# Eighty sampling steps in one pipeline, an expert network in tiles of chosen rows, one attention pipeline for all batches

## The reference

```python
x = x + deformable_attention(ctx, layernorm(x))   # 16 heads of 8, 5 points per head
x = x + moe0(layernorm(x))        # 32 experts of width 96, top 4 by sigmoid score + bias
x = x + attention1(layernorm(x), ctx)             # softmax over 154 tokens, then a norm
x = x + moe1(layernorm(x))        # 8 experts of width 512, top 2 by 20 Sinkhorn iterations

def moe0(x):                                       # all 2048 tokens
    scores = sigmoid(x @ gate_w.T)
    ids = top_k(scores + e_bias, 4)
    w = scores[ids] / sum(scores[ids])
    return sum over e: (silu(x @ w1[e]) * (x @ w3[e]) * combine[:, e]) @ w2[e]
```

## Time and profile before

| what | us |
|---|---|
| median of 3 runs | 1264.88 (1264.18 to 1271.11) |
| the profiled execution's own time | 1261.6 |
| its span, first to last instruction | 1259.7 |
| PE busy | 868.3 (69%) |
| DVE busy | 784.9 (62%) |
| ACT busy | 414.7 (33%) |
| POOL busy | 307.0 (24%) |
| mean granted TensorE clock | 0.843 of full |

### The profile page before, as it was taken

How to read it: one execution, slowest core, us unless ns; L and a number is a source line. 1 busy time by engine, 2 the same in 40 slices (tenths; PEclk the granted TensorE clock), 3 DMA queues, 4 the chain that set the end, 5 groups by cost and what they waited for, 6 DMA issues and landing times.

```text
span 1259.7 us, 13989 instructions
## 1 busy us (share of the span) xinstructions
PE 868.3 (69%) x4534; PEld 493.6 (39%) x4534; DVE 784.9 (62%) x1888; ACT 414.7 (33%) x731; POOL 307.0 (24%) x287
## 2 busy tenths in 40 slices
PE   4276589775689977667998667699684233269993
PEld 2022345322355432235554223454342122158883
DVE  2767655787776467777647686764583766744434
ACT  1122212133424633342463334336442111124441
POOL 2822100332600033250003134200100900036662
PEclk9988689988779997887999788699978555579997
DMA  6254000164000016500000750000050000001114
GB/s 218 86 187 148 16 0 1 55 214 161 13 3 1 1 37 218 176 1 16 1 1 21 233 174 3 4 1 1 26 183 9 1 0 1 0 23 41 43 43 117
DMA packets 45893, 77.94 MB, mean 62 GB/s; under 512 B 6599, under 2 KB 30413, under 8 KB 45438
## 3 DMA queue, kind: packets, MB, share of 16 engines
q1 hardware_dynamic: 43326, 71.91, 17.2%
q0 software_dynamic: 2496, 5.12, 1.5%
HBM read 71.76 MB, written 5.24 MB: 61 GB/s over the span
## 4 chain that ended last, share of the span: by engine, by line
PE 52%; DVE 30%; ACT 8%; issue 4%; DMA 3%; POOL 1%; SPq 1%; another core or an unknown queue 0%; DVEq 0%; POOLq 0%; PEldq 0%; ACTq 0%
PE PS L1280 6%; PE PS L1289 5%; PE PS L1402 5%; PE PS L1294 4%; DVE oh L954 4%; PE PS L1397 3%; PE PS L1661 3%; PE PS L1411 3%; PE PS L1639 2%; DVE oh L955 2%; PE PS L1302 2%; DMA oh<-index 2%; PE PS L1644 2%; DVE pkr L914 2%; PE PS L1516 1%
## 5 line engine op out<-in xcount | busy, mean ns | idle before, releaser
L1397 PE MATMUL PS<-oh,T 128*128 128x512 bf16 x240 | 80.5, 453 | 121.8 <-DVE oh L954 121.7
L794 DVE TENSOR_TENSOR sg<-sg,PS 128x512 f32<-128x512 f32 x96 | 66.0, 687 | 135.3 <-ACT sg L592 76.4
L617 ACT COPY gs<-PS 128x512 f32<-128x512 f32 x80 | 46.8, 585 | 233.0 <-PE PS L1402 233.0
L592 ACT ACTIVATE sg<-PS 128x512 f32<-128x512 f32 x96 | 57.4, 598 | 185.4 <-PE PS L1289 184.7
L1280 PE MATMUL PS<-hh,wd 128*128 128x512 f32 x192 | 109.0, 650 | 1.9 <-DVE hh L798 1.9
L1402 PE MATMUL PS<-oh,T 128*32 128x512 bf16 x960 | 80.4, 449 | 7.2 <-DVE oh L955 7.2
L955 DVE TENSOR_SCALAR oh<-oh,pcol 128x2048 bf16<-128x2048 bf16 x80 | 82.5, 1032 | 0.0
L1397 PEld LDWEIGHTS PS<-oh,T 128*128 128x128 bf16 x240 | 23.3, 108 | 147.5 <-issue 114.3
L455 POOL CAST T<-xnT 128x512 bf16<-128x512 f32 x8 | 5.4, 677 | 309.7 <-DVE xnT L878 309.7
L954 DVE TENSOR_SCALAR oh<-oh,pcol 128x512 bf16<-128x512 bf16 x80 | 66.1, 826 | 20.1 <-DMA oh<-index 20.0
L798 DVE TENSOR_TENSOR hh<-sg,PS 128x512 f32<-128x512 f32 x96 | 66.0, 687 | 3.3
(11 more groups left out here) (316 smaller groups left out, 2094.9 us busy)
## 6 DMA issues: line engine op xcount, KB each, us to landing
oh<-index SPq DMA_DIRECT2D x80, 512.0 KB, 3.6
oh<-index SPq DMA_DIRECT2D x80, 128.0 KB, 4.5
wg1r<-in_wg SPq DMA_DIRECT2D x8, 256.0 KB, 5.5
wu1r<-in_wu SPq DMA_DIRECT2D x8, 256.0 KB, 5.7
wd<-in_wd SPq DMA_DIRECT2D x8, 256.0 KB, 5.9
zb<-zrows SPq DMA_DIRECT2D x8, 256.0 KB, 4.8
wg0r<-in_wg SPq DMA_DIRECT2D x1, 1536.0 KB, 7.0
wu0r<-in_wu SPq DMA_DIRECT2D x1, 1536.0 KB, 10.2
```

The costliest lines, as they stand in the source:

```text
L592: act.activation(sg[:, j % 2, :], PS[:, 0, :], ACT.Silu).then_inc(s["sg_ready"], 1)
L794: dve.tensor_tensor(sg[:, j % 2, :], sg[:, j % 2, :], PS[:, 1, :], ALU.mult).then_inc(s["h_used"], 1)
L1397: pe.matmul(o, T2[:, p, g, :], oh[:, slot, GH, :], start=(p == 0), stop=False, skip_group_check=True)
```

## The change

It takes the stages out of the turns and runs each over all batches, with no loop and no meeting of the engines.

- **One sampling pipeline.** 80 steps in a row. In the 20 steps of batch b each engine also does `prep` of batch b+1 (slots 0 to 16) and `post` of batch b-1 (slots 9 to 21: projection, norm, scores, top 4, ranks, positions). Square roots become Exp(-0.5 Ln), the sigmoid an Exp and a reciprocal. POOL only multiplies the values by their weights, for every group, timed by `pt_used`; DVE reduces them (`combine`). At the end of `post`, POOL scatters each batch's normed rows four times into `xs`, a DRAM array with a region for each expert (16 indirect DMAs a batch).
- **The first expert network in tiles.** `route` and `pe_ffn` go. SP first writes 128 zero rows behind each expert's last row, at an address it loads into a register, 32 times. DVE and PE make a table of 96 tiles (8192 rows / 128, and 32 for part-filled tiles), always all of them. They pass in 48 pairs: PE turns the pair's rows (x0), ACT and DVE split them in a high and a low part, gate and up are 2 x 3 fp32r products of 192 columns, then Silu, one product, two transposes, two down products with 96 rows, a copy (y0), and a store to `ys`. SP loads with a register address into eight x0 buffers. PE loads four registers a pair. The expert's weights are one array `w0` (gate and up side by side, 32 x 192 columns), split once.
- **One attention pipeline.** Keys and values of all four batches are made first. Then 72 slots, r from -10 to 61, with a batch's scores every 12 slots; queries, norms, output turns and costs have slots of their own and share bank 4 (`SIDE`). POOL gathers each batch's 4 results per token from `ys` (16 indirect DMAs), weighs and adds them (batch 0's are added by DVE), and goes on splitting queries. The copy L1068 moves from DVE to ACT.
- Behind that, the code is the same, with five gather buffers for six; the second network's weights are loaded after the last group's output rather than during the tail.

The diff, cut to its core (`...` for what is left out):

```diff
--- before.py
+++ after.py
...
+STEPS = NG * NK
+ALL_STEPS = B * STEPS
...
+T0 = K0 * TOKENS // P + E0
+REGION = TOKENS + P
+XS_ROWS = E0 * REGION + T0 * P
+PAIRS = T0 // 2
+XB0, YB0 = 8, 4
...
+PERIOD = 3 * NG
+FRONT_FIRST, BACK_LAST = -10, 25
+MAX_FIRST = -4
+Q_SLOTS = {-7: 0, -5: 1, -4: 2, -2: 3}
...
+        def steps():
+            for g in range(ALL_STEPS + STEPS + POST_LAST + 1 - STEPS):
+                yield g
+
+        def parts(g):
+
+
+            b, n = divmod(g, STEPS)
+            preps = [(b + 1, n)] if b + 1 < B and n < PREP_SLOTS else []
+            posts = [(b - d, n + STEPS * (d - 1)) for d in (2, 1) if 0 <= b - d < B and n + STEPS * (d - 1) <= POST_LAST]
+            return preps, posts
...
+            spare = xs[E0 * REGION:E0 * REGION + E0 * P].rearrange("(c p) d -> p c d", p=P)
+            sp.dma_start(spare, nil[:].unsqueeze(1).to_broadcast([P, E0, D])).then_inc(s["fill_out"], 16)
...
+            store_index(0)
+            for g in range(ALL_STEPS):
+                b, n = divmod(g, STEPS)
+                if n == INDEX_STEP and b + 1 < B:
+                    store_index(b + 1)
+                spread(g)
+                if g == 2:
+                    sp.dma_start(w0r[:], a["w0"]).then_inc(s["experts0_in"], 16)
+                    sp.dma_start(wd0[:], a["wd0"]).then_inc(s["experts0_in"], 16)
...
+            def load_tile(i):
+                row = sp.value_load(tabi[0:1, 0, i:i + 1], min_val=0, max_val=XS_ROWS - P)
+                sp.dma_start(x0[:, i % XB0, :], xs[bass.ds(row, P)]).then_inc(s["xa_in%d" % (i % XB0 // 2)], 16)
+
+            sp.wait_ge(s["filled"], 1)
+            for e in range(E0):
+                row = sp.value_load(efilli[0:1, e:e + 1], min_val=0, max_val=XS_ROWS - P)
+                sp.dma_start(xs[bass.ds(row, P)], nil[:]).then_inc(s["fill_out"], 16)
+            sp.wait_ge(s["fill_out"], 16 * (E0 + 1))
+            for j in range(2):
+                sp.wait_ge(s["xs_out%d" % j], 16 * K0 * NT // 2)
+            sp.wait_ge(s["table_in"], 1)
+            for i in range(XB0):
+                load_tile(i)
+            for m in range(PAIRS):
+                sp.wait_ge(s["y0_ready"], m + 1)
+                for i in (2 * m, 2 * m + 1):
+                    sp.dma_start(ys[i * P:(i + 1) * P], y0[:, i % YB0, :]).then_inc(s["ys_out%d" % (i % YB0 // 2)], 16)
+                for i in (2 * m + XB0, 2 * m + 1 + XB0):
+                    if i < T0:
+                        sp.wait_ge(s["x0_ps"], (i - XB0) // 2 + 1)
+                        load_tile(i)
...
+            def weigh_values(q):
+                pool.wait_ge(s["coef_ready"], q + 1)
+                pool.wait_ge(s["vv_used"], NK * (q + 1))
+                if q + 1 < B * NG:
+                    pool.wait_ge(s["pt_used"], NK * (q + 2))
+                w = coef[:, q % 2].rearrange("p k s q -> p (k s q)").unsqueeze(2).to_broadcast([P, NK * 2 * QT * GH, HD])
+                v = vv[:, q % 3].rearrange("p k s q c -> p (k s q) c")
+                pool.tensor_tensor(v, v, w, ALU.mult).then_inc(s["vw_ready"], 1)
...
+            def scatter_rows(b):
+                pool.wait_ge(s["rows_made"], b + 1)
+                for t in range(QT):
+                    for k in range(K0):
+                        pool.indirect_dma_start(xs[:], bass.IndirectOffsetOnAxis(ap=row0[:, QT * b + t, k:k + 1], axis=0),
+                                                xn1[:, b % 2, t, :], None).then_inc(s["xs_out%d" % (b % 2)], 16)
...
+            def gather_results(b):
+                if b:
+                    pool.wait_ge(s["x2_ready"], b)
+                for t in range(QT):
+                    for k in range(K0):
+                        pool.indirect_dma_start(yb[:, b % 2, t, k, :], None, ys[:],
+                                                bass.IndirectOffsetOnAxis(ap=yrow0[:, QT * b + t, k:k + 1], axis=0))\
+                            .then_inc(s["yb_in%d" % t], 16)
...
+            def add_results(b):
+                for t in range(QT):
+                    pool.wait_ge(s["yb_in%d" % t], 16 * K0 * (b + 1))
+                y = yb[:, b % 2].rearrange("p t k d -> p (t k) d")
+                w = w0all[:, b * QT:(b + 1) * QT].rearrange("p t k -> p (t k)").unsqueeze(2).to_broadcast([P, QT * K0, D])
+                c.link(pool.tensor_tensor(y, y, w, ALU.mult))
+                y = yb[:, b % 2]
+                c.link(pool.tensor_tensor(y[:, :, 0:2], y[:, :, 0:2], y[:, :, 2:4], ALU.add))
+                c.link(pool.tensor_tensor(y[:, :, 0], y[:, :, 0], y[:, :, 1], ALU.add))
+                rows = XR[:, b * QT:(b + 1) * QT]
+                pool.tensor_tensor(rows, rows, y[:, :, 0], ALU.add).then_inc(s["x2_ready"], 1)
...
+            gather_results(0)
+            for r in range(FRONT_FIRST - 8, PERIOD * (B - 1) + BACK_LAST + 1):
+                for b in range(B):
+                    q = r - PERIOD * b
+                    if q in Q_SLOTS:
+                        split_query(b, Q_SLOTS[q])
+                    if q == -6:
+                        add_beta(b)
+                    if q == -16 and b:
+                        gather_results(b)
+                    if q == -12 and b:
+                        add_results(b)
+                    if q == 15:
+                        add_attention(b)
...
+            def high_pair(m):
+                act.wait_ge(s["x0_ps"], m + 1)
+                if m >= 2:
+                    act.wait_ge(s["gu_ps"], m - 1)
+                act.copy(x0h[:, m % 2, :], PS[:, 0, 0:2 * P]).then_inc(s["x0h_ready"], 1)
...
+            def combine(q):
+                b, g = divmod(q, NG)
+                dve.wait_ge(s["vw_ready"], q + 1)
+                if g == 0 and b:
+                    dve.wait_ge(s["post_ps"], post_use(b - 1, "ctxT") + 1)
+                dve.reduce_sum(ctok[:, :, g * GH * HD:(g + 1) * GH * HD],
+                               vv[:, q % 3].rearrange("p k s (t j) c -> p t (j c) (k s)", t=QT), AX_X).then_inc(s["comb_done"], 1)
...
+            def low_pair(m):
+                dve.wait_ge(s["x0h_ready"], m + 1)
+                if m >= 2:
+                    dve.wait_ge(s["gu_ps"], m - 1)
+                dve.tensor_tensor(x0l[:, m % 2, :], PS[:, 0, 0:2 * P], x0h[:, m % 2, :].bitcast(F32), ALU.subtract).then_inc(s["x0l_ready"], 1)
+
+            low_pair(0)
+            for m in range(PAIRS + 2):
+                if m + 1 < PAIRS:
+                    low_pair(m + 1)
+                if m < PAIRS:
+                    dve.wait_ge(s["s0_ready"], m + 1)
+                    if m >= 2:
+                        dve.wait_ge(s["hT0_ps"], m - 1)
+                    up = PS[:, 1 + m % 2, 0:4 * I0].rearrange("p (i v f) -> p i v f", i=2, v=2)[:, :, 1]
+                    dve.tensor_tensor(h0[:, m % 2], s0[:, m % 2], up, ALU.mult).then_inc(s["h0_ready"], 1)
+                if m >= 2:
+                    u = m - 2
+                    dve.wait_ge(s["y0_ps"], u + 1)
+                    if u >= YB0 // 2:
+                        dve.wait_ge(s["ys_out%d" % (u % (YB0 // 2))], 32 * (u // (YB0 // 2)))
+                    at = 2 * u % YB0
+                    dve.tensor_copy(y0[:, at:at + 2, :], PS[:, 5 + u % 2, 0:2 * P].rearrange("p (i d) -> p i d", i=2)).then_inc(s["y0_ready"], 1)
+
...
+            def turn_pair(m):
+                if m >= 1:
+                    pe.wait_ge(s["x0l_ready"], m)
+                pe.wait_ge(s["xa_in%d" % (m % (XB0 // 2))], 32 * (m // (XB0 // 2) + 1))
+                for i in (2 * m, 2 * m + 1):
+                    last = pe.transpose(PS[:, 0, (i % 2) * P:(i % 2 + 1) * P], x0[:, i % XB0, :], ident[:])
+                last.then_inc(s["x0_ps"], 1)
+
+            turn_pair(0)
+            down_cols = []
+            for m in range(PAIRS + 2):
+                if m + 1 < PAIRS:
+                    turn_pair(m + 1)
+                if m < PAIRS:
+                    up_cols = [pe.value_load(tabi[0:1, 1, i:i + 1], min_val=0, max_val=(E0 - 1) * 2 * I0) for i in (2 * m, 2 * m + 1)]
+                    pe.wait_ge(s["x0h_ready"], m + 1)
+                    pe.wait_ge(s["x0l_ready"], m + 1)
+                    if m >= 2:
+                        pe.wait_ge(s["h0_ready"], m - 1)
+                    for i in range(2):
+                        xh, xl = x0h[:, m % 2, i * P:(i + 1) * P], x0l[:, m % 2, i * P:(i + 1) * P]
+                        o = PS[:, 1 + m % 2, i * 2 * I0:(i + 1) * 2 * I0]
+                        w = bass.ds(up_cols[i], 2 * I0)
+                        pe.matmul(o, xh, w0h[:, w], start=True, stop=False)
+                        pe.matmul(o, xh, w0l[:, w], start=False, stop=False)
+                        last = pe.matmul(o, xl, w0h[:, w], start=False, stop=True)
+                    last.then_inc(s["gu_ps"], 1)
+                if 1 <= m <= PAIRS:
+                    u = m - 1
+                    pe.wait_ge(s["h0_ready"], u + 1)
+                    if u >= 2:
+                        pe.wait_ge(s["hT0_ready"], u - 1)
```

(27 more changed lines are left out.)

2095 lines of the change are left out of this document (1003 added, 1092 removed).

## The result

The changed kernel takes 1574.56 us (median of 4, 1565.1 to 1578.85) against 1267.27 us (median of 4) for the kernel before: a ratio of 1.2413, with a 95% interval from 1.2342 to 1.2483. The forecast was 1505, range 1385 to 1600. The time lies in the range, 4.6% above the forecast. The profiled execution took 1578.85 us, its span 1577.0.

The account below looks back on a forecast made before the run. It took TensorE (52% of the chain) and VectorE (30%) to bound the kernel. Terms 49 + 357 + 36 + 44 + 472 + 263 + 281 gave a 1502 us span, forecast 1505, range 1385 to 1600.

Parts of the forecast that it names:

- The pairs: First expert network's 48 tile pairs: TensorE waits for loads behind stores, 10.2 us a pair, 472 us in all.
- The first rival: In the 48 pairs: loads land before TensorE asks, 4.3 us a pair, total 1248 us, 1% faster; chance 0.08.
- Register loads: In pairs and passage: TENSOR_LOAD 0.30, whole load about 0.6 us; the skill's floor would add 53 us to the sum.
- the passage: From routing to the tiles: SyncE's 32 zero writes at 1.25 us each, landing and first loads, 44 us.
- The sampling: 80 sampling steps over four batches: VectorE sets the pace, 88.5 + 96.5 + 96.5 + 75 = 357 us.
- The weights ahead of the index rows: In the sampling: 4.5 MB of weights loaded ahead of the index rows, charged 5 us once.
- The second rival: In the sampling: GpSimd late, scatters held to 2.4 us beside comparisons, VectorE waits, total 1600 us; chance 0.10.
- Routing of the last batch: After the last sampling step: nothing covers the last batch's routing, 36 us.
- Attention: Attention over four batches: keys, gathers and GpSimd's additions every 48 us, then remaining slots and the end, 263 us.
- The rest: Everything behind the attention: keeps its code but for one gather buffer fewer, 281 us.
- The third rival: In the sampling: TensorE's half clock binds, 111 us a batch interlocked, total 1564 us; chance 0.10.
- The last: Rival without a place in the kernel: the change does less than it says, a pipeline stalling elsewhere hides the ring; chance 0.03.

Follow-up runs that it names:

- e1: Changed kernel with SyncE issuing the loads of pair m+6 before it waits for y0_ready of pair m, stores behind: 1299.54 us.
- e7: Changed kernel with ten x0 row buffers instead of eight (five pairs), order on SyncE unchanged: 1334.25 us.
- e6: Changed kernel with the attention's 16 indirect gathers a batch replaced by four plain loads of consecutive rows (other tokens' rows): 1522.48 us.
- e5: Changed kernel with all 64 scatters behind the last batch's routing, reading the last batch's rows: 1573.95 us.
- e4: Changed kernel with the 16 scatters of batch 2 moved behind the weighing of the last group: 1562.12 us.
- e11: e10 with VectorE instead of GpSimd adding the results of every batch in the attention: 1203.50 us.
- e2: Changed kernel with six gather buffers instead of five in the second expert network: 1547.52 us.
- e8: Kernel before the change with five gather buffers instead of six in the second expert network: 1296.72 us.
- e12: e1 with TensorE's four register loads a pair replaced by constant weight columns (wrong experts): 1256.08 us.
- e3: Changed kernel with the attention's gathers issued ahead: batch 1's behind batch 0's, batch b+1's after batch b is added: 1560.54 us.
- e9: Changed kernel with the edits of e1 to e4 together and the first network's weights loaded in 16 pieces over steps 18 to 33: 1229.67 us.
- e10: e9 with every second one of the 32 zero writes issued by ScalarE instead of SyncE: 1214.39 us.

## Why the prediction was right, and where not

**The pairs (472, measured 455.7)**: right in mechanism and nearly in size. TensorE's idle time was put at 5.5 and is 5.1, its own iteration at 4.7 and is 4.8, the period at 10.2 and is 9.9. The sum of that 4.7 is nearer than its terms: the six products start 0.21 apart and take 1.4 in all, not 2.0, and the register loads leave the array idle for 0.9, not 0.5. e1 and e7 show the cause: order alone removes it, one more pair halves the period. The first rival, the ring not tight, had its place right, "the wait for xa_in"; it failed because nothing in SyncE's program ran ahead. Its price was too high: a loose pair costs 3.89, not 4.3. e1 gives 1299.5 where the rival said 1248; the difference is the other terms, which it took over.

**Register loads.** I took the row's 0.30 for the instruction and 0.6 for a whole register load with what decodes it. The Trainium skill gives `tensor_load` a floor of about 600 ns (DMA: Bandwidth & Descriptors, Latency and other measured facts). The instruction alone lies under that floor, 0.30 us on TensorE and 0.27 on SyncE; the whole load does not, since two in a row start 0.64 apart on TensorE. The 0.30 more a load that I drew from the Trainium skill's figure did not come. On SyncE (ns min, median, max; first and last start):

```profile
L443 SPq TENSOR_LOAD <-efilli x32: 2/269/476, 473.6 to 508.9; - x32
L443 SPq FUSED_REGOPS  x32: 152/152/181, 474.1 to 509.2; - x32
```

A zero write with its register load comes every 1.09 us (median; mean 1.13), against my 1.25, and the passage is 41.6 against 44.

**The sampling (357, measured 373.3)**: the pace by VectorE is right (busy 290 of 373, and on one chip the term is 355). By batches it took 89.6, 89.7, 105.9 and 88.1 against 88.5, 96.5, 96.5 and 75. The step that failed is the last batch's 75 and the third's 96.5: TensorE's idle time near the scatters is not among my terms. Where it doesn't appear (e6, e7) these batches take 97 and 82 us, and without any scatters (e5) 93 and 77. The weights ahead of the index rows were charged 5 and cost 16 (27.9 against 12.1 us for the first five steps), and only other idle time that was charged and didn't come, in batches 0 and 1, hides that.

**The second rival, GpSimd late**: not as it was put. It had each scatter held by the comparisons to 2.4 us; 64 scatters have a median of 0.97 and a mean of 1.06, and only two of its three bursts lie in the sampling. What the Trainium skill tells of a copy (SBUF — State Buffer, A bandwidth-pool intuition that's wrong) shows here beside a few long operations, none of them a copy: 6.93 us for one scatter in e4 beside a subtraction of 6.54, and at most 2.41 in the changed kernel, in the passage, beside an operation of 2.29 on two tensors. But the place where GpSimd was late is real, and I missed it.

**Routing of the last batch (36, measured 55.7)** is the step that failed there. It said that nothing covers this stage, and summed VectorE's work. It did not ask what GpSimd had in its queue ahead of the last product: the scatters of batch 2, 20 us. e4 without them measures 38.1; the sum of the work was right.

**Attention (263, measured 293.3)**: to the first maximum 48.6 and not 59, from the gathers' start to the addition's end 31 as forecast (32); but batches came 58 apart and not 48. The step that failed there is the stretch from one addition's end to the next gathers, for which 48 leaves 16: it takes 27. e6, without indirect gathers, still needs 40 to 48 a batch, and e11, with the gathers ahead and the additions on VectorE, has its first maxima 48.2, 49.5 and 44.3 apart; no run has both gathers and additions off GpSimd, so what the slots alone need isn't shown. The other half of the miss is the end of the stage, from the last addition on: 90 where I had 60 and 16. Some 7 of these 14 are TensorE's lower clock in the last 36 us (last section); the other 7 are open.

**The rest (281, measured 313)**: the step "keeps its code but for one gather buffer fewer", costed at nothing. I had the rule in hand, from the pairs: how long after a buffer is free does its next content land, and how many iterations lie between. Here scatter, gather and landing, 1.3, 1.0 and 2.6, follow the copy of tile i, and with five buffers the tile that needs them is one iteration away. e2 and e8 give 30 us of the stage for it.

**The third rival, the half clock binding the sampling**, fell: the granted clock there is 0.80, and VectorE is the busier. **The last**, less than it says, fell too: 48 pairs run.

**In sum**, the 75 us of span that the forecast lacks are routing 20, attention 30, second network 32 and sampling 16, less 23 in the start, the passage and the pairs. That is why the time lies near the upper end of the range, and 23 us of errors the other way helped to keep it there. The largest share, and routing's, come from stages whose queues on GpSimd I did not write out tile by tile, as I had done for SyncE's.

## What to carry to other kernels

For each ring of buffers, write down which event frees a slot, which instructions of the in-order queue stand between it and the transfer that refills it, and how many iterations later the content is wanted: one instruction order cost 266 us of the stage here, and one buffer fewer, in the kernel before and after alike, 30. Issue the loads of an iteration ahead of any wait for its results. When a change leaves a stage "as it is" but takes a buffer from it, the stage isn't as it was.

## What the runs showed of the hardware that was not expected

- Near the end of each burst of 16 indirect DMAs of GpSimd, TensorE stood some 2 to 7 us without a visible reason in the samplings of nine kernels (in e12 3 at most), on two chips at least; on another the same code showed none (e6, e7). e5, which has no scatters there and no stand, ran on that other chip, so it doesn't prove that they cause it. The mechanism is open, and whether it belongs to the chip wasn't tried.
- A scatter of GpSimd beside VectorE's operation of 2.29 us on two tensors took 2.41 us in the passage; one that ran wholly beside a reduction of 2.29 us took 0.97, as without any.
- With the loads ahead, TensorE was busy 93% of the stretch of the pairs and the granted clock stayed at 0.52, the lower of its two levels. Without register loads between its matrix instructions it was busy 74% and the clock 0.73 (e12). Why the busier stretch has the lower clock, no run here settles.
- The same instructions at the end of the attention, from the third batch's last addition to the fourth's, took 36 us in the changed kernel, e2, e4 and e11, 31 in e3, e9 and e10, and 29 in e1, e5, e6, e7 and e12. The granted clock tells them apart: 0.59 or 0.60, 0.83, and 0.85. The rows below are the changed kernel's and e1's. In the changed kernel two products of the attention take 2.07 us from the tenth microsecond of the stretch on, in e1 the same two take 1.13. In the 20 us before the stretch TensorE was busy 16.4 and 16.5 us, so that doesn't tell them apart, and no run here settles why the clock fell.

```profile
1220.00:1256.10 36.10, 21.99 (x72) 9.28 (x70) 10.12 (x50) 8.12 (x14) 2.56 (x3) 0.59 0.09 30
```

```profile
947.50:976.70 29.20, 14.91 (x72) 6.49 (x70) 10.16 (x49) 8.09 (x14) 2.52 (x2) 0.85 0.12 37
```
